# Second convolution of a residual chain: partial shifts in 32x32 float32 tiles, and a whole copy of its input

## The reference

```
x = x + conv(x, W0, groups=4, pad=4) + (c @ C0.T)[:, :, None] + bias     # x: (32, 128, 2048) float32
x = x + einsum('boi,bih->boh', sum_k att1[b, k] * M1[k], x) + (att1 @ b1)
x = x + einsum('boi,bih->boh', sum_k att2[b, k] * M2[k], x) + (att2 @ b2)
x = x + conv(x, W3, groups=4, pad=4) + (c @ C3.T)[:, :, None] + bias
# att = softmax(MLP(c)) over 8 matrices
```

## Time and profile before

| | us |
|---|---|
| median of 3 runs | 631.91 |
| lowest, highest | 631.85, 632.3 |
| the profiled execution, whole | 635.33 |
| its span | 633.5 |
| TensorE busy in it | 622.8 |
| VectorE busy | 500.9 |
| ScalarE busy | 338.2 |
| GpSimd busy | 272.3 |

### The profile page before, as it was taken

One profiled execution on the slowest core, in us unless ns is written; L12 is line 12 of the kernel. 1 busy time (PEld: TensorE's weight loads), 2 busy tenths in 40 slices (PEclk: granted clock), 3 DMA queues, 4 the chain that ended last, 5 costly groups with the idle time before them and its releaser, 6 DMA issues.

```text
span 633.5 us, 26750 instructions
## 1 busy us (share of the span) xinstructions
PE 622.8 (98%) x11938; PEld 506.3 (80%) x11938; DVE 500.9 (79%) x1002; ACT 338.2 (53%) x626; POOL 272.3 (43%) x163
## 2 busy tenths in 40 slices
PE   8999999999999999999999999999999999999995
PEld 6888897777788777889877778777878877788874
DVE  6899777978777887887887887797877788788735
ACT  4665455555455456455456446555545545645534
POOL 4133454354355345355435345435435534534220
PEclk8999999999999999999999999999999999999998
DMA  8066665557765556775555776555776555655515
GB/s 244 24 188 215 203 211 177 204 163 225 232 207 156 190 176 199 232 232 158 173 191 175 232 232 182 158 202 162 223 232 208 155 190 176 201 169 168 161 76 201
DMA packets 50572, 118.84 MB, mean 188 GB/s; under 512 B 5621, under 2 KB 26282, under 8 KB 42714
## 3 DMA queue, kind: packets, MB, share of 16 engines
q1 hardware_dynamic: 49170, 116.04, 58.1%
q0 software_dynamic: 576, 1.26, 0.5%
q10 hardware_dynamic: 776, 0.89, 0.4%
HBM read 35.33 MB, written 33.55 MB: 109 GB/s over the span
## 4 chain that ended last, share of the span: by engine, by line
PE 96%; DMA 2%; DVE 1%; ACT 1%; issue 0%; ACTq 0%; DVEq 0%
PE ps L1068 45%; PE ps L1079 19%; PE ps L1090 16%; PE ps L1214 14%; PE ps L1192 1%; DMA out_sb<-in_L_cond_weight 1%; DMA out_planes<-out_taps 1%; ACT out_sb L740 1%; PE ps L1262 0%; PE ps L1185 0%; DVE out_taps L856 0%; DVE x_in L950 0%; DVE x_hi L993 0%; PE ps L1250 0%; PE ps L1302 0%
## 5 line engine op out<-in xcount | busy, mean ns | idle before, releaser
L513 POOL COPY out_sb<-out_planes 128x2048 f32<-128x2048 f32 x30 | 123.0, 4099 | 187.8 <-issue 162.0
L496 POOL COPY x_full<-x_in 128x2048 f32<-128x2048 f32 x29 | 117.1, 4038 | 113.9 <-DVE x_lo L822 110.1
L846 DVE SCALAR_TENSOR_TENSOR z_lo<-ps,bias_tab,z_hi 128x1024 fp32r<-128x1024 f32 x62 | 76.7, 1279 | 60.7 <-ACT z_hi L649 60.7
L1090 PE MATMUL ps<-x_full,taps_raw 32*32 32x512 f32 x2880 | 102.2, 598 | 0.0
L1068 PEld LDWEIGHTS ps<-z_hi,taps_hi 32*128 32x128 f32 x1488 | 71.0, 183 | 35.4 <-issue 25.1
L1068 PE MATMUL ps<-z_hi,taps_lo 32*128 32x512 f32 x1488 | 96.5, 387 | 0.0
L836 DVE SCALAR_TENSOR_TENSOR y_lo<-ps,bias_tab,y_hi 128x512 fp32r<-128x512 f32 x128 | 87.2, 744 | 10.2 <-ACT y_hi L639 10.2
L1068 PE MATMUL ps<-z_hi,taps_hi 32*128 32x512 f32 x1488 | 94.2, 396 | 0.0
L657 ACT ACTIVATE out_taps<-ps,bias_tab 128x512 f32<-128x512 f32 x62 | 39.3, 685 | 102.2 <-PE ps L1068 102.2
L1068 PE MATMUL ps<-z_lo,taps_hi 32*128 32x512 f32 x1488 | 90.3, 385 | 0.0
L1214 PE MATMUL ps<-y_hi,mix_w 32*128 32x512 f32 x1024 | 88.0, 385 | 0.0
(11 more groups left out here) (158 smaller groups left out, 831.0 us busy)
## 6 DMA issues: line engine op xcount, KB each, us to landing
x_in<-in_x SPq DMA_DIRECT2D x31, 1024.0 KB, 5.3
out_planes<-out_taps SPq DMA_DIRECT2D x122, 256.0 KB, 3.6
out<-out_sb SPq DMA_DIRECT2D x30, 1024.0 KB, 4.6
mix_w<-prod SPq DMA_DIRECT2D x124, 128.0 KB, 4.0
x_in<-in_x SPq DMA_DIRECT2D x2, 512.0 KB, 5.9
out<-out_sb POOLq DMA_DIRECT2D x2, 512.0 KB, 3.5
out<-x_full SPq DMA_DIRECT2D x7, 128.0 KB, 2.9
out_taps<-in_L_cond_weight SPq DMA_DIRECT2D x1, 512.0 KB, 5.8
```

The lines of the kernel that those rows point to most:

```text
L496: pool.tensor_copy(row_order(t, d, x[:, :, home(t, d)]), x_order(t, d, x_in[t.par(d)][:, :])).then_inc(x_planed, 1)
L513: pool.tensor_copy(x_order(t, d, out_sb[t.par(d)][:, :]), row_order(t, d, out_planes[:, :, :]))\
L846: dve.scalar_tensor_tensor(out=z_home(t, 0)[1][:, 2 * h:2 * h + 2, home(t, 0)], in0=ps[:, k:k + 2, :], scalar=bias_tab[:, b, 2 * G:BIAS], ...
L1090: tile = pe.matmul(ps[rows(p), first_bank + g, :], taps_raw[l][rows(g), d - p, :], full[rows(g), d % PH, c:c + S], start=False, stop=(n == ...
```

## The change

The last convolution of samples 1 to 30 is made like the first: `conv3_mixed` starts with `partial_turns` on a new whole buffer z_full, and then runs the 18 whole turns, 4 of them (LATER) before the product (in step 31: before the mixing) and 14 behind. Its partial block stands directly behind that of the first convolution of the next sample, since `conv0_mixed` now ends a step's first half. The waits for z_lo_done and z_full_edged are put into `conv0_mixed`, before its last two whole shifts (eight matmuls). ScalarE writes z_full in `whole_z`, between the row copies of z_hi and those of z_lo: two reads of PSUM of 1024 columns, each behind the z_lo of the same half, and two row copies of 3 phases by 63. The row copies of z_hi and z_lo shrink to one phase each.

The order of the output rows in PSUM changes with it from channel-major to phase-major, since a 32x32 tile writes 32 neighbouring partitions; the bias columns and the relay's source partitions follow. Sample 31 keeps the old order: its taps are rebuilt in the buffers of the first convolution (zeroed by GpSimd once that has ended for good, filled by ScalarE and VectorE in step 31 ahead of z_hi and z_lo), and its bias is laid out by four small DMAs from GpSimd's queue in step 16.

```diff
+        def full_z(t, d):
+            return not isinstance(t.half, int) or FIRST_FULL_Z <= t.i + d < N - 1
...
-                    sp.dma_start(out_planes[:, p, :], out_taps[p:C:PH, :, :]).then_inc(out_relaid, DMA)
+                    sp.dma_start(out_planes[:, p, :], out_taps[rows(p), :, :]).then_inc(out_relaid, DMA)
...
             def edges_z(t):
                 for z, done in ((z_hi, z_hi_done), (z_lo, z_lo_done)):
+                    if z is z_lo and full_z(t, 0):
+                        whole_z(t)
                     act.wait_ge(done, 2 * (t.i + 1))
-                    for o, i in edges(z):
+                    for o, i in (edges(z, slice(PH - 1, PH), slice(0, 1)) if full_z(t, 0) else edges(z)):
                         last = act.activation(o, i.bitcast(F32), ACT.Copy)
                 last.then_inc(z_edged, 1)
+
+            def whole_z(t):
+                b = t.i
+                for h in range(2):
+                    act.wait_ge(z_lo_done, 2 * b + h + 1)
+                    k = bank(t, 0) + 2 * h
+                    act.activation(z_full[:, 2 * h:2 * h + 2, home(t, 0)], ps[:, k:k + 2, :], ACT.Identity,
+                                   bias=bias_tab[:, b, 2 * G:BIAS]).then_inc(z_full_done, 1)
+                act.wait_ge(z_full_done, 2 * (b + 1 - FIRST_FULL_Z))
+                for o, i in full_edges(z_full):
+                    last = act.activation(o, i, ACT.Copy)
+                last.then_inc(z_full_edged, 1)
...
                 if t.at(N - 1):
+                    last_taps_high()
                     high_z(t)
...
                 if t.at(N - 1):
+                    last_taps_low()
                     low_z(t)
...
-                whole_turns(bank(t, 0), 0, hi, lo, [(2, d) for d in far], step, False)
+
+                pe.wait_ge(z_lo_done, 2 * b)
+                pe.wait_ge(z_full_edged, b - FIRST_FULL_Z)
+                if t.at(2):
+                    pe.wait_ge(taps_raw_step[1], 2)
+                whole_turns(bank(t, 0), 0, hi, lo, [(2, d) for d in far], step)
                 if middle:
                     middle()
-                partial_turns(bank(t, 0), 0, full, conv0_done, step)
+                partial_turns(bank(t, 0), 0, full, step, done=conv0_done)
+
+            def conv3_mixed(t, turns, middle):
+                b = t.i - 1
+                order = [(k, d) for k in range(2) for d in WHOLE] + [(2, d) for d in WHOLE]
+                if t.at(2):
+                    pe.wait_ge(prod_summed, b + 2)
+                partial_turns(bank(t, -1), 1, z_full, BLK, first=True)
+                pe.wait_ge(z_edged, b + 1 - PLAIN)
+                whole_turns(bank(t, -1), 1, z_hi, z_lo, order[:turns], BLK)
+                middle()
+                whole_turns(bank(t, -1), 1, z_hi, z_lo, order[turns:], BLK, done=conv3_done)
...
-            LATER = 20
+            LATER = 4
...
-                mid = MID + 4 if t.at(2) else MID if t.at(N - 1) else LATER
-                if t.has(-1):
-                    conv3(t, -1, range(mid))
-                if t.has(1):
-                    product(t, 1)
-                if t.at(N - 1):
-                    mix(t)
-                if t.has(-1):
-                    conv3(t, -1, range(mid, TURNS))
-                if t.has(0) and not t.at(N - 1):
+                elif t.at(N - 1):
+                    conv3_mixed(t, LATER, lambda: mix(t))
+                else:
+                    conv3_mixed(t, LATER, lambda: product(t, 1))
                     mix(t)
```

More of the change, by code:

```diff
@@ L46 @@
 FIRST_MIXED = 2
+FIRST_FULL_Z = 1
 K = 8
@@ L584, in _, with bias_for_last, zero_last_taps @@
             first_planes(ALL[1], 1)
+            def bias_for_last():
+                pool.wait_ge(bias_tab_done, 3)
+                for p in range(PH):
+                    pool.dma_start(bias_last[p:C:PH, :], bias_tab[rows(p), N - 1, G:2 * G]).then_inc(bias_last_in, DMA)
+            def zero_last_taps():
+                pool.wait_ge(conv0_done, G * N)
+                for w in (taps_hi[0], taps_lo[0]):
+                    pool.memset(w[:, :, :].bitcast(F32), 0.0).then_inc(last_taps_zeroed, 1)
             for t in ALL[2:N]:
@@ L664, in taps_high, with last_taps_high @@
                    .then_inc(taps_hi_done[l], 1)
+            def last_taps_high():
+                act.wait_ge(last_taps_zeroed, 2)
+                for p in range(PH):
+                    act.activation(last_columns(taps_hi, p), taps_raw[1][:, :, :], ACT.Copy).then_inc(last_taps_hi_done, 1)
             def spread_first():
@@ L940, in one, with last_taps_low @@
                     low_z(t)
+            def last_taps_low():
+                dve.wait_ge(last_taps_zeroed, 2)
+                for p in range(PH):
+                    dve.wait_ge(last_taps_hi_done, p + 1)
+                    dve.tensor_tensor(out=last_columns(taps_lo, p), in0=taps_raw[1][:, :, :],
+                                      in1=last_columns(taps_hi, p).bitcast(F32), op=ALU.subtract)\
+                       .then_inc(last_taps_lo_done, 1)
             def turn_last(h):
@@ L1071, in conv_turns, with whole_turns @@
                             tile.then_inc(done, 1)
-            def whole_turns(first_bank, l, hi, lo, turns, step, first):
+            def whole_turns(first_bank, l, hi, lo, turns, step, first=False, done=None):
                 for k, d in turns:
@@ L1078, in whole_turns, with partial_turns @@
                     for g in range(G):
-                        pe.matmul(ps[:, first_bank + g, :], w[rows(g), d, :], a[rows(g), d % PH, c:c + S],
-                                  start=(first and (k, d) == turns[0]), stop=False)
-            def partial_turns(first_bank, l, full, done, step):
+                        tile = pe.matmul(ps[:, first_bank + g, :], w[rows(g), d, :], a[rows(g), d % PH, c:c + S],
+                                         start=(first and (k, d) == turns[0]), stop=(done is not None and (k, d) == turns[-1]))
+                        if done is not None and (k, d) == turns[-1]:
+                            tile.then_inc(done, 1)
+            def partial_turns(first_bank, l, full, step, first=False, done=None):
                 for n in range(PARTIAL):
@@ L1090, in partial_turns @@
                             tile = pe.matmul(ps[rows(p), first_bank + g, :], taps_raw[l][rows(g), d - p, :],
-                                             full[rows(g), d % PH, c:c + S], start=False, stop=(n == PARTIAL - 1))
-                        if n == PARTIAL - 1:
+                                             full[rows(g), d % PH, c:c + S], start=(first and n == 0),
+                                             stop=(done is not None and n == PARTIAL - 1))
+                        if done is not None and n == PARTIAL - 1:
                             tile.then_inc(done, 1)
@@ L1104, in conv0_mixed @@
                 wait(pe, out_dve, 2 * (b - 1))
-                whole_turns(bank(t, 0), 0, hi, lo, [(k, d) for k in range(2) for d in near], step, True)
+                whole_turns(bank(t, 0), 0, hi, lo, [(k, d) for k in range(2) for d in near], step, first=True)
                 if not plain(t, 0):
                     pe.wait_ge(x_hi_edged, b + 1 - PLAIN)
-                whole_turns(bank(t, 0), 0, hi, lo, [(k, d) for k in range(2) for d in far], step, False)
+                whole_turns(bank(t, 0), 0, hi, lo, [(k, d) for k in range(2) for d in far], step)
                 if not plain(t, 0):
```

46 lines of the change are left out of this document (30 added, 16 removed).

## The result

The changed kernel is slower: median 688.96 us (687.74 to 690.69, 4 runs) against 632.05 us (631.85 to 632.3, 4 runs), a ratio of 1.0902 with a 95% interval of 1.0877 to 1.0927. The sign was forecast, the size was not: 653 (638 to 668) was said, so that +21 us became +57.

A forecast was written before the change was run, and what follows sets the result against it. TensorE's instruction stream was taken as the bound; the span 633.5 + 30 x 0.65 + 1 + 0.7 = 654.7 us, less 1.6 from span to median, gave 653 us, range 638 to 668 for 8 in 10.

The forecast's parts named there:

- What bounds the kernel: TensorE, busy for 622.8 us of a 633.5 us span; a change counts where it shortens its stream or makes it stand.
- the stall: TensorE waits for z_full before the first convolution's last 8 whole matmuls, T+3.63 to T+5.66: 2.1 us a step (1.8 to 2.3).
- five intervals of 0.875 and one last round of 1.59 make 5.97 us: Time claimed for six rounds of 32x32 tiles, x's and z's partial blocks back to back, against 3.34 for three.
- rival (c): Each 32x32 tile block costs its full 3.34 us, 6.68 for two instead of 5.97: 674 us; chance 0.06.
- the restart after the wait: TensorE starting again after the z_full wait with a weight load that nothing hides: 0.07 us added to the stall.
- The gain of 1.45: TensorE time saved a step: new last convolution and both partial blocks take 10.45 us, before it was 11.90.
- Net of a step: Stall less gain in each loop step: 2.1 - 1.45 = +0.65 us, to 19.47.
- rival (d): TensorE's clock falls to half for 6.8 us, costing 3.4 us, in every third step: 687 us; chance 0.08.
- Product and y_lo: Product before mixing waits for y_lo: y_lo done at T+12.6, product due at T+13.3, so no stall.
- The terms that come once: Step 2's wait behind the product's sum, +1 us, and sample 31's last convolution waiting for z_lo, +0.7 us.
- the predicted span of 654.7: Forecast profiled span of the whole kernel: 633.5 + 30 x 0.65 + 1 + 0.7 us.

## Why the prediction was wrong in size

- **What bounds the kernel, and the stall: right.** z_full was put at T+5.66, it came at T+5.67; the stall was 2.1 us in the sum and is 5.81 - 3.63 = 2.18. z_lo (T+3.87 said, T+3.88 read) and VectorE's last matrix (T+8.1, 352.04 read) came where they were put.
- **The step that failed: "five intervals of 0.875 and one last round of 1.59 make 5.97 us".** It took 6.58. The rows gave the pace of three rounds behind whole matmuls, and I extended it to rounds behind rounds. A round of 64 instructions took 0.87 us in the first block and 1.06 in the second, as long as the second stood directly behind. What the earlier trace rows showed as waits between bursts was the array's pace. There was a sign of another limit behind it that I did not follow: the bursts of loads grow from 0.55 to 0.75 us within rounds of 0.87. At the least the sum should have had a wider bound here: two blocks at 3.34 each, rival (c)'s 6.68, is close to what came. Rival (c) named a change of mode between the blocks as the cause. That isn't what happens, the 0.84 us pause comes once. The step alone is 29 x 0.61 = 17.7 us of the miss.
- **The rest of the gain:** entering the tiles behind the stalled matmuls took 0.67 us, where 0.57 was said, and the restart after the wait 0.14 (with T+5.67 to T+5.81) instead of 0.07. The gain of 1.45 is thus (4.08 of whole matmuls, less 3.24 for z's block) 0.84, less 0.1. Net of a step: +1.41 in the one shown and +1.425 on average, not +0.65. That is 29 x 0.775 = 22.5 us of the miss. With it alone the forecast would have been 675.6, already outside of 638 to 668.
- **The clock: rival (d) came in part,** and the sum had nothing for it. I took the time for which the clock held after the last matmul (3.2 us) as a reason against a fall at 2.1 us. Of the 25 steps from 6 to 30 five fell. A fall cost 1.5 us, not the 3.4 of (d), as it lasted 3.4 us and not 6.8. The Trainium skill, "TensorE: Matmul & The Clock Gate", HAM oscillation, tells of a recurring wait for a DMA that threw the clock back each time. The changed kernel agrees in one step of five, the run with two waits in a step in all from 5 to 30; the run with the blocks apart has no such wait in its loop and no fall there (clock 1.00). Why one step falls and the next does not stays open: their rows are alike up to the wait's end. It is not chance from step to step, though: the falls of steps 7, 13, 19 and 25 begin 122.9 us apart, every sixth step.
- **Missing instructions: not foreseen.** 0.9 and 1.6 us in steps 4 and 5.
- **Product and y_lo: right in that nothing waits.** y_lo ended at T+13.17 and the product issued at T+14.09, 0.92 us behind it (0.7 said); both came later than said (T+12.6 and T+13.3), as the tiles ended later.
- **The terms that come once** were too small. I gave step 2 and the end +1.7 together. Step 2 is 1.1 us over the net of a step, where 1 was said, but that is luck: the stall doesn't add to the chain of the product's sum, which waits for the product only and lets mixing start without a wait (VectorE's timeline, first line below). What makes the step longer is half clock for 3.4 us. The end took 1.6 over a step's net (3.02 - 1.42). Of this 0.58 come before the last convolution's start, where 0.7 was said, with the wait for x_lo, which there holds sample 31's z_lo, in it (TensorE's timeline, second line). The other 1.0 come behind its start, 0.8 of them behind the last matmul, and I have not traced them further.

```profile
64.56 0.69 DVE L951 TENSOR_REDUCE prod_sum<-ps 128x128 f32<-128x512 f32 x1 [1.33 <-PE ps L1272]
...
671.17 1.74 PE L1253 MATMUL ps<-x_hi,taps_hi 32*128 32x256 f32 x48 [0.54 <-DVE x_lo L899]
```

With these, the predicted span of 654.7 becomes 654.7 + 22.5 (steps) + 13.6 (longer steps, 14.6 less the 1 foreseen) + 1.7 (3.02 less 1.35 foreseen) - 3.6 (start) = 688.9, which is the span read.

What is shown, and what is argued: that z's block is slow only directly behind x's, and not by its buffer or by PSUM readers, is shown by the runs with the blocks apart and with z's block last. That it is the supply of instructions is argued from two rows, the gap "issue" inside the block and the bursts behind it. The Trainium skill, "TensorE: Matmul & The Clock Gate", in its section Architectural detail, gives TensorE a queue of 64 entries from which weight loads are pulled ahead. Bursts of 32 loads in 0.23 us with as many matmuls between them agree with a full one. No run varied the supply itself while keeping the blocks together, except the written-out loop, which made the gaps longer. And one stretch doesn't fit easily. In the run with y's reading put off, x's first two rounds ran at half clock and took 1.70 us each, longer than the 1.06 in which 64 instructions came; they should have got ahead in that time (weight loads of x's block; those of z's, from 298.56, stand above):

```profile
294.27 0.28 PEld L1156 LDWEIGHTS ps<-x_full,taps_raw 32*32 32x32 f32 x32 [0.37 <-issue]
...
295.97 0.64 PEld L1156 LDWEIGHTS ps<-x_full,taps_raw 32*32 32x32 f32 x31 [0.68 <-issue]
...
297.68 0.67 PEld L1156 LDWEIGHTS ps<-x_full,taps_raw 32*32 32x32 f32 x30 [0.68 <-issue]
```

Yet z's block behind them, at full clock again, was as even as ever. Why eight whole matmuls bring the bursts back and two slow rounds do not stays open.

## What to carry to other kernels

A wait costs what stands behind it on its engine: put it directly ahead of the first instruction that needs it, or bring work that doesn't need it in front. The second way took the same idea from 9% slower to 1.4% faster. A pace read from a short block of very short instructions holds for that length and its surroundings only; bound the price of a second block from above by a whole block. Long matmuls between two such blocks bring the pace back but not the time: apart they took 6.66 us, together 6.58. When a part of a queue's order is moved, follow the slack on both sides: two turns later for the product cost 12 us.

## What the runs showed of the hardware that I had not expected

- TensorE took 32x32 matmuls and their weight loads at 1.06 us for 64 instructions (16.6 ns each) directly behind another such block, and at 0.87 us behind 8 matmuls of 32x128.
- An idle time of 2 us on TensorE was followed by half clock for 3.4 us in five of 25 steps that were otherwise alike.
- Writing out a loop of 24 steps cost 9.2 us: 99 instead of 31 packets of instructions, and gaps of up to 1.6 us between TensorE's matmuls (2.3 and 2.4 in the two runs with a late wait), with some of them followed by half clock.
- A DMA out of 32 neighbouring partitions took 4.7 us to land where one whose source is every fourth partition took 3.6, and the loads of x beside it went from 5.3 to 7.5.
